# A ring of 16 pairs of gathered tiles instead of 17, with six pairs fetched row by row from the sync queue

## What is computed

```python
xn = layernorm(x)
# gnn: the aggregation is a sum over the edges of each node
h = norm * (xn @ W.T + bias)              # norm = rsqrt(1 + number of edges of the node)
agg = segment_sum(h[dst], src, 6250)      # a gather of 100000 rows, summed by source node
gnn = norm * (agg + h)
# mix: linear attention over all nodes (keys' softmax, one context per head), gated, projected
x = x + gnn + mix(xn)
# ffn: for the 3124 nodes of largest router weight: gelu(z @ w1 + b1) @ w2 + b2, times the weight
z = layernorm(x)
x = x + ffn(z)                            # + z
```

## Time and profile before

| | us |
|---|---|
| median of 3 runs | 1396.64 (1394.07 to 1398.44) |
| the profiled execution | 1397.45 |
| its span, first to last instruction | 1395.7 |
| mean granted clock of TensorE, share of full speed | 0.934 |

### The profile page before, as it was taken

How to read it: one execution, slowest core, us unless ns; L and a number is a source line. 1 busy time by engine, 2 the same in 40 slices (tenths; PEclk the granted TensorE clock), 3 DMA queues, 4 the chain that set the end, 5 groups by cost and what they waited for, 6 DMA issues and landing times.

```text
span 1395.7 us, 27723 instructions
## 1 busy us (share of the span) xinstructions
PE 1109.0 (79%) x6477; PEld 808.6 (58%) x6478; DVE 990.7 (71%) x3564; ACT 373.4 (27%) x1168; POOL 813.0 (58%) x879
## 2 busy tenths in 40 slices
PE   0499999999877888888888888878887878778853
PEld 0388887888654555555555566546555555445532
DVE  7999999999456666666666665666665666566667
ACT  5844466665411111111111111111111111111100
POOL 0110003542776777777777777777777777777710
PEclk9789999999988999999999999999999999999976
DMA  9100301333643344333434443434434443344315
GB/s 228 33 2 2 106 26 55 104 103 93 183 114 103 117 120 120 117 113 119 118 118 118 118 120 109 120 117 120 117 112 120 118 119 114 116 120 118 112 30 184
DMA packets 76390, 149.81 MB, mean 107 GB/s; under 512 B 17983, under 2 KB 48415, under 8 KB 75707
## 3 DMA queue, kind: packets, MB, share of 16 engines
q0 software_dynamic: 37536, 102.55, 25.4%
q1 hardware_dynamic: 17190, 25.56, 6.5%
q10 hardware_dynamic: 21606, 21.05, 5.1%
HBM read 132.83 MB, written 12.80 MB: 104 GB/s over the span
## 4 chain that ended last, share of the span: by engine, by line
POOL 28%; PE 24%; issue 15%; DVE 10%; DMA 3%; DVEq 2%; ACT 1%; SPq 0%; POOLq 0%; ACTq 0%
POOL gath L460 28%; PE bank L840 7%; PE bank L770 3%; PE bank L778 3%; PE bank L762 3%; PE bank L896 3%; DMA gath<-table,col_of 2%; PE bank L885 2%; DVE onehot L1301 2%; DVE big_g L1500 1%; PE bank L863 1%; DVE rs L1355 1%; PE bank L855 1%; DVE rs L1357 1%; DVEq L1301 1%
## 5 line engine op out<-in xcount | busy, mean ns | idle before, releaser
L460 POOL DMA_INDIRECT gath<-table,col_of x782 | 752.8, 963 | 269.3 <-issue 251.7
L840 PE MATMUL bank<-gath,onehot 128*128 x916 | 295.1, 423 | 111.5 <-SPq L377 55.2
L1301 DVE TENSOR_SCALAR onehot<-iota_b,row_of,minus_row 128x128 bf16 x916 | 253.7, 328 | 107.6 <-issue 72.6
L840 PEld LDWEIGHTS bank<-gath,onehot 128*128 x916 | 89.0, 97 | 315.0 <-DVE onehot L1301 147.6
L885 PE MATMUL bank<-vv,w_sb 128*128 128x125 f32 x1600 | 201.7, 287 | 0.9 <-ACT vv L626 0.9
L640 ACT ACTIVATE WT<-bank,norm 125x256 f32<-125x256 f32 x50 | 23.7, 473 | 661.1 <-PE bank L847 661.1
L885 PEld LDWEIGHTS bank<-vv,w_sb 128*128 128x128 f32 x1600 | 194.8, 202 | 1.9 <-ACT vv L626 1.7
L896 PE MATMUL bank<-w_sb,keyB 128*125 128x256 f32 x800 | 184.6, 384 | 0.0
L1331 DVE SCALAR_TENSOR_TENSOR WT<-bank,norm,WT 125x256 f32<-125x256 f32 x50 | 24.2, 484 | 197.3 <-ACT WT L640 192.2
L896 PEld LDWEIGHTS bank<-w_sb,keyB 128*125 128x125 f32 x800 | 147.7, 190 | 19.9
L632 ACT ACTIVATE keyB<-bank,b_sb 128x125 f32<-128x125 f32 x400 | 113.0, 366 | 161.0 <-PE bank L885 161.0
(11 more groups left out here) (298 smaller groups left out, 1542.0 us busy)
## 6 DMA issues: line engine op xcount, KB each, us to landing
gath<-table,col_of POOLq DMA_INDIRECT x782, 2.8
w_sb<-in_x ACTq DMA_DIRECT2D x50, 125.0 KB
parts<-table ACTq DMA_DIRECT2D x50, 125.0 KB
h_s<-in_x ACTq DMA_DIRECT2D x50, 125.0 KB
big_g<-in_x SPq DMA_DIRECT2D x5, 1120.0 KB
out<-big_g SPq DMA_DIRECT2D x8, 560.0 KB
table<-parts SPq DMA_DIRECT2D x30, 112.0 KB
table<-Wqc SPq DMA_DIRECT2D x20, 112.0 KB
```

The costliest lines, as they stand in the source:

```text
L460: g.indirect_dma_start(out=gath[:, tile % NB, :], out_offset=None, in_=table[:, :], in_offset=bass.IndirectOffsetOnAxis(ap=col_of[:, tile: ...
L840: last = t.matmul(bank[0][:, 0:PART], onehot_g[:, hot_slots, u * 128:(u + 1) * 128].rearrange("p a r -> p (a r)"), gath_g[:, slots, u * PA ...
L1301: last = nc.vector.tensor_scalar(onehot_g[:, slots, u * 128:(u + 1) * 128].rearrange("p a r -> p (a r)"), iota_b[:, :], row_of[:, bass.ds( ...
```

## The change

Pairs q with q % 65 == 64 that belong to the first six periods (64, 129, 194, 259, 324, 389) are **own pairs**. POOL passes over them. SP fetches their 256 rows one by one into the last two tile places of `gath`, which are no longer part of the ring: the ring is `RING` = 16 pairs. The row numbers come from `own_rows`, a buffer of six rows of 256 numbers in the first partitions of the place of `Wg2_b`, which is not used any more by then; six copies before the loop turn the columns of `col_of` into it. The rows are spread over the period: after each pair from the first to the 62nd SP issues 4 or 5 of them (in the first period it begins at q = 8, so 256 rows fall on 54 pairs). For 8 rows it loads 8 registers, and for each row it computes the address and issues one transfer of 1 KB. Two pairs ahead of the own pair it waits for all 256 rows and copies the two tiles (256 KB) into their ring place; at the own pair it waits for that copy (`staged`) instead of `s_block`.

`LAG` becomes 8: at pair q SP waits for the sums of pair q - 8 and then frees up to pair `RING + q - 8`. The index of a ring place is q % 16 on PE too.

```diff
--- before.py
+++ after.py
@@ -40,7 +40,7 @@
 NROUND = NBLK // ROUND
 assert NROUND * ROUND == NBLK
 PAD_ROW = NODES + 3 * NW - 1
-LAG = 3
+LAG = 8
 NXR = 4
 DUE_MAX = 32000
 LEVELS_IN_GROUP = 5
@@ -66,6 +66,12 @@
 SEARCH = sum(STEPS)
 FREED_BY = 4
 FREED_ALONE = 2 * ROUND
+RING = ROUND - 1
+PERIOD = 65
+NOWN = NBLK // PERIOD
+OWN_UNTIL = PERIOD - 4
+COPY_AHEAD = 2
+AT_ONCE = 8
 NB_KT = 2
 PEEK_FROM, PEEK, PEEK_LEAD = 10, 12, -26
 PEEK_DEALT, KMAX_AFTER = 10, 16
@@ -199,6 +205,7 @@
         gate_tmp = sb("gate_tmp", [128, NBLK])
         hg = gate_tmp[0:P, 2 * P:2 * P + 2 * GH].rearrange("p (j n) -> p j n", j=2)
         due_row = gate_tmp[0:1, :].bitcast(I32)
+        own_rows = Wg2_b[0:NOWN, :].bitcast(I32)
         table_of = sb("table_of", [P, 1])
         hgT = gate_tmp[0:GH + 1, 0:2 * P].rearrange("p (j n) -> p j n", j=2)
         kmax = sb("kmax", [128, 2])
@@ -258,9 +265,9 @@
...
-        s_block = [sem(f"s_block{k}") for k in range(ROUND)]
+        s_block = [sem(f"s_block{k}") for k in range(RING)]
...
@@ -279,6 +286,13 @@
         held_at = (NW * HCH // 2 + 63) // 64 * 64
         held.append(gath[:, :, :].rearrange("p s c -> p (s c)").bitcast(F32)[:, held_at:held_at + 8 * 2 * P])
         assert held_at + 8 * 2 * P <= (NB - 6) * C
+
+        def is_own(q):
+            return q % PERIOD == PERIOD - 1
+
+        def gathered_into(q):
+
+            return sum(not is_own(n) for n in range(q % RING, q + 1, RING))
 
         def turned_x(m, ahead=1):
 
@@ -363,7 +377,7 @@
                 table_rows(m)
 
             sp.wait_ge(s["tabs"], 1)
-            sp.sem_inc(s["freed"], ROUND)
+            sp.sem_inc(s["freed"], RING)
 
             sp.wait_ge(s["due"], 1)
             sp.wait_ge(s["gate"], NW)
@@ -371,16 +385,53 @@
             sp.wait_ge(s["xnr"], NW)
             sp.dma_start(w2_sb[:, :, :], w2.rearrange("(c p) n -> p c n", p=128)).then_inc(s["wdown"], 16)
             sp.wait_ge(s["duerow"], 16)
-            freed = ROUND
+            sp.wait_ge(s["tabs"], 2)
+            with nc.allow_non_contiguous_dma(reason="row numbers of one block, two from each partition"):
+                for k in range(NOWN):
+                    q = k * PERIOD + PERIOD - 1
+                    sp.dma_start(own_rows[k:k + 1, :].rearrange("a (p u) -> a p u", u=GROUP),
+                                 col_of[:, q * GROUP:(q + 1) * GROUP]).then_inc(s["turned"], 16)
+            rows = [sp.alloc_register(f"own_row{n}") for n in range(AT_ONCE)]
+
+            def gather_own(k, lo, hi):
+
+                for n in range(lo, hi):
+                    if n % AT_ONCE == 0:
+                        sp.load(rows, own_rows[k:k + 1, n:n + AT_ONCE])
+                    row = sp.snap(rows[n % AT_ONCE], min_val=0, max_val=NODES - 1)
+                    sp.dma_start(gath[n // GROUP:n // GROUP + 1, RING * GROUP + n % GROUP, :],
+                                 table[bass.ds(row, 1), :]).then_inc(s["own"], 16)
+
+            freed, given = RING, 0
             for q in range(NBLK):
-                sp.wait_ge(s_block[q % ROUND], 16 * GROUP * (q // ROUND + 1))
+                k, at = divmod(q, PERIOD)
+                if is_own(q):
+                    sp.wait_ge(s["staged"], 16 * (k + 1))
+                    given = 0
+                else:
+                    sp.wait_ge(s_block[q % RING], 16 * GROUP * gathered_into(q))
                 sp.sem_inc(s["arrived"], 1)
-                free = ROUND + q + 1 - LAG
+                free = RING + q + 1 - LAG
                 if freed < free and freed < NBLK and (q < FREED_ALONE or q % FREED_BY == 0):
                     due = sp.value_load(due_row[0:1, q:q + 1], min_val=1, max_val=DUE_MAX)
                     sp.wait_ge(s["visits"], due)
                     sp.sem_inc(s["freed"], free - freed)
                     freed = free
+                if k < NOWN:
+                    first = LAG if k == 0 else 0
+                    if q == first:
+                        sp.wait_ge(s["vdone"], 1)
+                        sp.wait_ge(s["turned"], 16 * NOWN)
+                    if first <= at <= OWN_UNTIL:
+                        upto = GEDGE * (at + 1 - first) // (OWN_UNTIL + 1 - first)
+                        gather_own(k, given, upto)
+                        given = upto
+                    if is_own(q + COPY_AHEAD):
+                        to = (q + COPY_AHEAD) % RING
+                        sp.wait_ge(s["own"], 16 * GEDGE * (k + 1))
+                        assert freed > q + COPY_AHEAD
+                        sp.dma_start(gath[:, to * GROUP:(to + 1) * GROUP, :],
+                                     gath[:, RING * GROUP:(RING + 1) * GROUP, :]).then_inc(s["staged"], 16)
             for lo, hi in out_groups:
                 sp.wait_ge(s["final"], hi)
                 sp.dma_start(out_v[0:SPRAY, lo:hi, :], big_g[0:SPRAY, lo:hi, :]).then_inc(s["outs"], 16)
@@ -455,12 +506,14 @@
                     g.wait_ge(s["tabs"], 2)
                 if q == ROUND - 6 // GROUP:
                     g.wait_ge(s["vdone"], 1)
+                if is_own(q):
+                    continue
                 g.wait_ge(s["freed"], q + 1)
                 for tile in range(q * GROUP, (q + 1) * GROUP):
                     g.indirect_dma_start(
-                        out=gath[:, tile % NB, :], out_offset=None, in_=table[:, :],
+                        out=gath[:, tile % (RING * GROUP), :], out_offset=None, in_=table[:, :],
                         in_offset=bass.IndirectOffsetOnAxis(ap=col_of[:, tile:tile + 1],
-                                                            axis=0)).then_inc(s_block[q % ROUND], 16)
+                                                            axis=0)).then_inc(s_block[q % RING], 16)
 
         @block.scalar
         def _(a):
@@ -832,10 +885,10 @@
 
                 with counted(t, f"sums{next(loops)}", first, end) as (q, upto):
                     made = q + before
-                    for value in (made, q % ROUND, made % HOTS):
+                    for value in (made, q % RING, made % HOTS):
                         t.compute_val(value)
                     t.wait_ge(s["arrived"], upto)
-                    slots, hot_slots = bass.ds(q % ROUND, 1), bass.ds(made % HOTS, 1)
+                    slots, hot_slots = bass.ds(q % RING, 1), bass.ds(made % HOTS, 1)
                     for u in range(GROUP):
                         last = t.matmul(bank[0][:, 0:PART],
                                         onehot_g[:, hot_slots, u * 128:(u + 1) * 128].rearrange("p a r -> p (a r)"),
```

More of the change, by code:

```diff
@@ L260, in gps_layer @@
                  "moved kT kmaxd cntd kmt kmx kmr kv ekv xnr ctxp sumcp sumtp sumtc vdone ctxn wqcp wqcd pads ranked dealt oh arrived visits freed due duerow selfused "
-                 "op og pp xb xm sum xh low x1 st nt zed ge zwt ztp zT hp gelu yp yv base halves csum").split()
+                 "op og pp xb xm sum xh low x1 st nt zed ge zwt ztp zT hp gelu yp yv base halves csum own staged turned").split()
         s = {n: sem("s_" + n) for n in names}
-        s_block = [sem(f"s_block{k}") for k in range(ROUND)]
+        s_block = [sem(f"s_block{k}") for k in range(RING)]
         s_xr = [sem(f"s_xr{j}") for j in range(NXR)]
```

## The result

The changed kernel takes **1419.49 us** in the median (1417.48 to 1420.24, 4 runs); the kernel before, run beside it, 1396.56 us. The ratio is 1.0163, with a 95% interval of 1.0143 to 1.0183: 23 us slower. The forecast was 1394 us, with a range to 1412. The profiled execution took 1418.82 us, its span is 1417.1 us, 21.4 us more than before.

The account below looks back on a forecast made before the run. POOL's gathers were taken as the bound, the last one setting the end. Terms: -15.2 + 2.5 + 2.4 + 4.6 + 1.7 + 0.8 = -3.2 us, forecast 1394 us, range 1386 to 1412 us.

Parts of the forecast that it names:

- rival 2: SP between 381 and 470 us: rows at 0.43 to 0.49 us stop POOL, 1401 to 1414 us; chance 0.22.
- The row: SP's queue: register work and issue of one row transfer take 0.39 us, 0.23 us of it the issue.
- the load of registers: SP's queue, per 8 rows: a load with what waits for it costs 0.42 us, 0.25 us per pair.
- the release: SP's queue, freeing ring places for POOL: 0.7 us each, one per pair for q from 8 to 33.
- SP keeps up from q = 34 on: SP against POOL's 2.53 us per pair: 2.3 us later in the first 65 pairs, 2.05 in other periods.
- The cover until q = 24: SP's pairs 8 to 24, 16 x 2.80 us to 425.8 us, hidden by POOL's wait for block 15 until 427.3.
- The step after pair 33: SP's q = 33 to 36: next release after three pairs of rows, 7.2 us instead of 2.53, +4.6 us.
- The smaller ring: POOL's stop before 427.30 us: with 16 pairs, not 17, it issues one pair later, +2.5 us.
- The lag of eight: SP waits for block q - 8, not q - 3; the waits that go are on no path, 0 us.
- The copies: 256 KB copies into the ring, landing in 3.5 us; only the last, pair 389, delays the end, +0.8 us.
- rival 3: SP becomes the bound in all periods, from 0.5 us per row; at 0.56 us 1480 us or more; chance 0.08.
- The rival that PE bounds: PE or DVE bounds, so POOL's chain isn't shortened; excluded down to -33 us, PE ending at 1304 us at the earliest.

Follow-up runs that it names:

- experiment 4: Changed kernel with registers loaded once per own pair (6 loads, not 192), so each own pair gets the same eight rows repeatedly: 1393.77 us.
- experiment 6: Changed kernel with each load filling 4 registers instead of 8 (384 loads, not 192): 1461.78 us.
- experiment 1: Changed kernel with no own pairs, only the ring of 16 pairs and lag of eight; POOL gathers all 782 tiles: 1400.91 us.
- experiment 10: Changed kernel with pair 64 gathered by POOL (five own pairs) and the lag back at three: 1514.78 us.
- experiment 7: Changed kernel with the odd rows of each own pair fetched by one transfer of 128 fixed rows, all loads kept: 1387.43 us.

## Why the prediction was wrong

The frame held: the last gather sets the end, a stop of POOL counts in full, and the twelve gathers are worth 15.2 us. The case that came true is rival 2, "SP's start-up pace costs more than the gathers save", which had 22%, but at a size beyond its own end, and not by the row issues on which it was made to hang. Step by step:

- **The row, 0.39 us: nearly right.** 0.41 us, of which the issue is 218 ns (0.23 taken). 4.8 rows per pair between pairs 9 and 34, not 4.74; together 0.12 us per pair.
- **The failed step is the load of registers, "0.42 us", and with it the release, "0.7 us".** Both were costed with a load of 268 ns, which reads one register in a queue that issues nothing. The load of eight registers took 782 ns, with what waits for it 0.81; the release's load, now behind row issues, 466 ns, the release 0.92. That is 0.24 and 0.22 us per pair, 0.46 of the 0.62 us by which 2.80 was too low. Experiments 4 and 6 show it from both sides: the loads nearly gone, 1394 us, by luck the forecast's own number; the loads doubled in count, 1462. The Trainium skill ("DMA: Bandwidth & Descriptors", Latency and other measured facts) gives a load of registers a floor of about 600 ns. The rows lie on both sides of it: 268 ns in the kernel before, 534 for eight registers in experiment 4, 782 behind issues.
- **"SP keeps up from q = 34 on" fell with it.** A pair there takes SP 0.6 x 0.81 = 0.49 us of loads instead of 0.25: 1.97 + 0.49 + 0.23 + 0.06 = 2.75 us against POOL's 2.53, so small stops went on through the first period, to 543 us, instead of ending after pair 40. In the other periods 4.13 x 0.41 + 0.42 + 0.23 + 0.06 = 2.40 us: SP keeps up, as forecast, with less room, and POOL waits for nothing there.
- **The cover until q = 24 didn't hold.** The rows began 2 us later than taken, at 383 us (SP waited 4.3 us for the turning copies), and 16 x 3.42 us end at 437.7, not 425.8: 10 us behind the 427.3 us at which block 15 had been summed before. The forecast said this cover ends at 0.40 us per row (by its own terms it is 0.41) and costs 0.8 us per 0.01 us; the same sum with 3.42 us in it gives 10.4 + 9 x 0.89 + 6.0 + 3.5 us, about 28, and small stops of about 7 after it: the 35.3 us that were found. The step after pair 33 was forecast at 4.6 us and took 5.96, the next 1.7 and took 3.4.
- **The smaller ring, +2.5 us.** Right by its mechanism, and in the change itself hidden behind SP. Where SP is quick enough for it to show (experiment 1) the stop is 1.2 us longer, half of the forecast, and the shorter lead adds 1.9 us.
- **The lag of eight, "0": wrongly told.** It costs nothing, but it isn't idle: without it the rows cost 126 us (experiment 10). The prediction priced it as a wait taken away and not as what lets SP work ahead.
- **The copies, +0.8 us.** Right: landing 3.3 us (3.5 taken), and 1.2 us more behind the last gather. SP waits up to 3.9 us for a landing, but no stop of POOL follows from it.
- **Pair 64 itself.** The gain of 2.5 us for an own pair holds only where POOL is the bound. The last stop, 3.2 us at 542.92 us, is where that of the first period went: passing over pair 64, POOL comes to its pair 65, which waits for SP's release at q = 60, after three pairs instead of four, while SP still takes four. No copy is in it; the first is issued at 549.2 us:

```profile
542.92 0.94 POOL L513 DMA_INDIRECT gath<-table,col_of  x1 [3.50 <-SPq L418]
...
L433 SPq DMA_DIRECT2D gath<-gath x6: 477/477/514, 549.2 to 1353.7; - x6
```

- **The rule of the Trainium skill** ("DMA: Bandwidth & Descriptors", Why a DMA increments its semaphore by 16 and not by 1) of 512 cycles, an estimated 0.43 us per issue, which would have made rival 3 true: the rows have 218 ns. The measurement decides. A kernel can come near rival 3 all the same, by its loads, as experiment 6 does.
- DMA engines, PE and DVE: 0, as said. The rival that PE bounds was rightly left out.
- **The signs.** The row spacing, 0.41 us, lay inside the 0.35 to 0.43 us that the forecast allowed; POOL's waits for SP after 500 us, which it named as a sign of being wrong, came. The load and the release had no sign of their own.
- **Slips in the working.** The range stops at 1412 us, though rival 2's own end is 1414. Rival 2 is 0.7 us less late at q = 24 than it says (16 x 3.04 us from 381 us end at 429.6). In rival 3 SP becomes the bound at about 0.52 us per row by the terms given, not 0.5. None of these decides the outcome.

What stays open: why a load takes 0.2 to 0.26 us more behind a row issue. It was seen with one, four, eight and sixteen registers, but no run took all the issues away while the loads stayed (with half of them, in experiment 7, a load takes 750 ns in the median).

## What to carry to other kernels

When work is given to a queue that has "time to spare", add up what the queue does between two events that others wait for, with each instruction costed in the place where it will stand, and compare it with the pace of the engine that waits; a surplus of waiting in lumps is no room for steady work. Look for the stretch in which that queue is already busiest (here the start, with a release per pair) and keep the new work out of it: leaving out one of six own pairs turned +23 us into -8. A lag or a lead that seems slack may be what allows the queue to work ahead, so it is tested together with the work, not by itself.

## What was not expected of the hardware

- A load into registers on SP costs by the register and by what is ahead of it: 268 ns for one with nothing ahead, 466 behind row issues; 534 and 782 ns for eight; 975 (the least) and 1236 for sixteen; 298 (the least) and 556 for four. Between eight and sixteen that is 57 ns per register.
- A register-addressed transfer of one row of 1 KB is issued in 218 ns in the median of 1536 (217 at the least, 331 at the most); the nearest rows of before, of 125 rows, had 264 to 270. With its register work a row takes 0.41 us of the queue.
- 1536 such transfers did nothing measurable to the gathers that ran beside them: POOL's gathers stay at 946 ns in the median, and with 1280 rows in the program the kernel was faster than before.
